# Three moves in a two-layer attention kernel: the last group of V's products in halves, half of the normalisation on ScalarE, output products from the last pair's third step

## The chip, the cores and the metric

The kernel runs on one core of a Trainium2 chip. The metric is the device time of one execution in microseconds (us), and lower is better. A core has TensorE (PE, matrix products into PSUM), VectorE (DVE), ScalarE (ACT), GpSimd (POOL) and SyncE (SP), which here only issues transfers. Each engine works off its own queue in order, and the engines meet at semaphores.

## The reference

Two layers run one after the other on x of 8 images, 512 channels and 32 x 32 places (T = 1024 tokens). Each is a group norm, a product for queries, keys and values, attention with 8 heads of 64, an output product, a bias and the residual. Cut to what matters:

```python
xn = group_norm(x, norm_w, norm_b)                 # 32 groups of 16 channels
q, k, v = split(qkv_w @ xn + qkv_b)                # per head: 64 channels each
weight = softmax(scale * q^T k)                    # 1024 x 1024 per image and head
a = weight @ v
out = x + proj_w @ a + proj_b
```

## The kernel before

**Passes.** One pass is one image in one layer, so the loop `Fori(0, PASSES)` runs 16 times on every engine. Within a pass the 8 heads go in 4 pairs. A head has 8 tiles of 128 queries, so a pair has 16 steps m = 0 to 15, one for each tile. Every fp32 product is made of three products of rounded parts (high by high, low by high, high by low), so operands are split into a high and a low part by ACT, POOL and DVE.

**One tile.** PE makes its scores (`scores`, L803 on, six matmuls, lines 812 and 814), DVE takes the row's smallest value (`smallest`, L600), ACT the exponential (`exponential`, L487), DVE the reciprocal of the row sum (L604), POOL multiplies by it (`normalise`, L373), PE transposes the tile (`transpose`, L823, eight matmuls into two halves of `ps_t`), ACT copies the high parts (`high_part`, L492), DVE subtracts for the low parts (`low_part`, L609), and PE weighs V with them (`weigh`, L835 and L836). PE's step with an even m first makes the scores of tiles m+2 and m+3. The scores of tile m+3 write the half of `ps_s` that the exponential of tile m+1 has read, so they wait for it.

**Start of a pass.** PE makes Q and K of head 0 (`qk_part`, 24 matmuls, channel block by channel block: block k waits for `xn_ready`), groups 0 to 3 of V (`values`, 12 matmuls each, one group for each 128 tokens), Q and K of head 1, and then groups 4 to 7 of V between the first scores. Group 7 stands between the transposes of tile 0 and those of tile 1 and goes to the bank `ps_o`. DVE copies each group out (`evac_v`, L673). ACT and POOL then split V for head 0 (`v_high` L481, `v_low` L367), and the first `weigh` waits for that.

**Boundary between passes.** Behind the last pair PE makes what is left of the eight output products (`project`, L775, in `OUT_ORDER`). Meanwhile DVE works out the group norm's coefficients of the next image (`norm_coefs`, ending at L663, `norm_b`). POOL then normalises the four blocks of 128 channels in place (`x_normalise`, L379), ACT copies each block's high part (`x_high`, L503), DVE subtracts for the low part (`x_low`, L668), and PE's next Q and K wait for it. Behind the four blocks ACT and POOL split blocks 2 and 3 of V's weights (`wv_high` L507, `wv_low` L346). Ahead of the first pass the same is written out by hand, and there ACT normalises blocks 1 and 3 (`x_normalise_first`, L516).

**Last pair.** In pairs 0 to 2 every step also makes three matmuls of the Q and K of a later head. The last pair has none to make. Its steps take the first nine matmuls of output product 6 instead, by the table `FILL`: step m makes the matmuls from the first to the second number. Step 4 first waits for the weights, for the last copy of Q and K out of the bank `ps_g`, which product 6 then fills, and for the attention of pairs 0 and 1. The scores of the last head (from tile 8 on, issued in step 6) wait for four transfers of its Q and K from one half of the partitions to the other (`stack`, L251 and L252). The loads of the next image are issued shortly before.

## Time and profile before

| | us |
|---|---|
| median of 3 runs | 4344.32 |
| lowest, highest | 4338.59, 4344.67 |
| the profiled execution's own time | 4335.69 |
| its span, first to last instruction | 4333.9 |

| engine | busy us | share of the span |
|---|---|---|
| PE | 4245.1 | 98% |
| DVE | 3305.3 | 76% |
| ACT | 2872.4 | 66% |
| POOL | 2436.4 | 56% |

The granted clock of TensorE is 0.999 of its full 2.4 GHz over the span. In the timelines a row begins with its start in us from the span's start and its duration; xN says that N neighbouring instructions of one kind are put together; brackets at the end give the idle time of the engine just before and what ended it. PEld is the weight load that runs ahead of a matmul.

### The profile page before, as it was taken

To read this page: it belongs to the slowest core of one execution; us is meant where nothing else is said; L and a number is where in the kernel's file an instruction comes from. 1 tells how busy PE (TensorE), PEld (TensorE's weight loads), DVE (VectorE), ACT (ScalarE), POOL (GpSimd) and SP (SyncE) were. 2 spreads that over 40 slices of the span, in tenths; PEclk is the share of its full clock that TensorE was granted. 3 is DMA by queue.
4 is the path that set the end of the run, shared out by engine and by line. 5 is a ranking of instruction groups with operands and counts; after the bars stand their busy time and mean duration, and the time that the engine had idled before them with its cause. 6 is when DMAs were issued, how large, how long until landed. Compare 5 with 4: busy or idle time off the path is not lost.

```text
span 4333.9 us, 94006 instructions
## 1 busy us (share of the span) xinstructions
PE 4245.1 (98%) x28740; PEld 3570.5 (82%) x28740; DVE 3305.3 (76%) x5479; ACT 2872.4 (66%) x5375; POOL 2436.4 (56%) x2332
## 2 busy tenths in 40 slices
PE   8999999999999999999999999999999999999999
PEld 6888888888887888878888788887888878888787
DVE  5878868688686886868868688686886868868687
ACT  4757747577574775747657476574765847658476
POOL 5646546465564655646566465564655646556464
PEclk9999999999999999999999999999999999999999
DMA  2121221212112121121221212122121211212112
GB/s 75 39 91 37 64 64 39 91 37 73 55 39 91 38 73 57 43 85 39 76 62 50 81 37 75 55 56 76 39 74 55 63 64 39 74 55 65 62 39 83
DMA packets 99645, 261.01 MB, mean 60 GB/s; under 512 B 15232, under 2 KB 15360, under 8 KB 99328
## 3 DMA queue, kind: packets, MB, share of 16 engines
q1 hardware_dynamic: 99328, 257.12, 20.0%
q8 instruction: 158, 2.59, 0.3%
q14 instruction: 159, 1.30, 0.1%
HBM read 122.84 MB, written 33.55 MB: 36 GB/s over the span
## 4 chain that ended last, share of the span: by engine, by line
PE 85%; POOL 4%; DVE 4%; issue 3%; DMA 2%; ACT 1%; SPq 1%; DVEq 0%; POOLq 0%; ACTq 0%
PE ps_t L823 20%; PE ps_s L812 17%; PE ps_g L775 15%; PE ps_o L835 10%; PE ps_o L836 10%; PE ps_s L775 6%; PE ps_t L775 4%; PE ps_o L775 2%; POOL x_raw L379 2%; DMA lo_sw<-lo_st 2%; PE ps_s L814 1%; DVE pt_lo L609 1%; DVE xn_lo L668 1%; POOL probs L373 0%; POOL v_st L367 0%
## 5 line engine op out<-in xcount | busy, mean ns | idle before, releaser
L373 POOL TENSOR_SCALAR probs<-probs,row_stats 128x1024 f32<-128x1024 f32 x1024 | 1153.0, 1126 | 1452.2 <-DVE row_stats L604 1452.1
L492 ACT CAST pt_hi<-ps_t 128x512 fp32r<-128x512 f32 x2048 | 1105.5, 590 | 759.6 <-PE ps_t L823 752.4
L600 DVE TENSOR_REDUCE row_stats<-ps_s 128x1 f32<-128x1024 f32 x1024 | 1249.2, 1220 | 296.5 <-PE ps_s L814 291.2
L609 DVE TENSOR_TENSOR pt_lo<-ps_t,pt_hi 128x512 fp32r<-128x512 f32 x2048 | 1317.3, 685 | 184.6 <-ACT pt_hi L492 171.8
L487 ACT ACTIVATE probs<-ps_s,row_stats 128x1024 f32<-128x1024 f32 x1024 | 1157.3, 1130 | 111.8 <-DVE row_stats L600 111.8
L823 PE MATMUL ps_t<-const_sb,probs 128*128 128x128 f32 x8192 | 1098.1, 276 | 5.1 <-POOL probs L373 4.8
L823 PEld LDWEIGHTS ps_t<-const_sb,probs 128*128 128x128 f32 x8192 | 898.6, 141 | 204.7 <-issue 179.5
L835 PE MATMUL ps_o<-pt_hi,v_st 128*128 128x256 f32 x4096 | 1023.6, 283 | 1.4
L836 PE MATMUL ps_o<-pt_lo,v_st 128*128 128x256 f32 x4096 | 1011.3, 281 | 0.0
L835 PEld LDWEIGHTS ps_o<-pt_hi,v_st 128*128 128x128 f32 x4096 | 770.1, 188 | 46.6 <-POOL v_st L367 8.3
L836 PEld LDWEIGHTS ps_o<-pt_lo,v_st 128*128 128x128 f32 x4096 | 772.0, 188 | 39.3
L812 PE MATMUL ps_s<-hi_sw,hi_st 64*128 64x512 f32 x1024 | 467.1, 456 | 44.5 <-DMA lo_sw<-lo_st 22.2
L814 PE MATMUL ps_s<-hi_st,hi_sw 64*128 64x512 f32 x1024 | 468.3, 457 | 0.0
L814 PE MATMUL ps_s<-hi_st,lo_sw 64*128 64x512 f32 x1024 | 405.2, 396 | 0.0
L812 PE MATMUL ps_s<-lo_sw,hi_st 64*128 64x512 f32 x1024 | 401.8, 392 | 0.0
L812 PE MATMUL ps_s<-hi_sw,lo_st 64*128 64x512 f32 x1024 | 399.3, 390 | 0.0
L814 PE MATMUL ps_s<-lo_st,hi_sw 64*128 64x512 f32 x1024 | 399.0, 390 | 0.0
L775 PE MATMUL ps_g<-xn_hi,wqk_hi 128*128 128x512 f32 x768 | 367.8, 479 | 0.0
L362 POOL TENSOR_TENSOR lo_st<-qk,hi_st 128x512 fp32r<-128x512 f32 x256 | 331.3, 1294 | 21.3
L812 PEld LDWEIGHTS ps_s<-hi_sw,hi_st 64*128 64x128 f32 x1024 | 188.2, 184 | 178.4 <-ACT probs L487 72.8
L775 PE MATMUL ps_g<-xn_hi,wqk_lo 128*128 128x512 f32 x768 | 305.2, 397 | 0.0
L775 PE MATMUL ps_g<-xn_lo,wqk_hi 128*128 128x512 f32 x768 | 301.8, 393 | 0.0
(125 smaller groups left out, 6397.3 us busy)
## 6 DMA issues: line engine op xcount, KB each, us to landing
wqk_raw<-in_wqk SPq DMA_DIRECT2D x130, 256.0 KB, 2.6
hi_sw<-hi_st SPq DMA_DIRECT2D x128, 256.0 KB, 3.1
lo_sw<-lo_st SPq DMA_DIRECT2D x128, 256.0 KB, 3.5
x_raw<-layer_out SPq DMA_DIRECT2D x36, 512.0 KB, 5.3
wv_raw<-in_wv SPq DMA_DIRECT2D x66, 256.0 KB, 5.2
x_raw<-in_x SPq DMA_DIRECT2D x32, 512.0 KB, 5.2
hi_sw<-hi_st SPq DMA_DIRECT2D x128, 128.0 KB, 3.1
lo_sw<-lo_st SPq DMA_DIRECT2D x128, 128.0 KB, 3.3
```

What stands on the lines that cost most here:

```text
L362: nc.gpsimd.tensor_tensor(lo_st[s][:, cols], qk[:, cols], f32(hi_st[s][:, cols]), ALU.subtract).then_inc(qk_split, 1)
L373: nc.gpsimd.tensor_scalar(probs[m % 2][:, :], probs[m % 2][:, :], row_rcp[:, m % 4:m % 4 + 1], 1.0, ALU.mult, ALU.mult).then_inc(probs_rea ...
L487: nc.scalar.activation(probs[m % 2][:, :], ps_s[:, m % 2, :], ACT.Exp, bias=row_min[:, m % 4:m % 4 + 1], scale=-1.0, accum_out=row_sum[:, ...
L492: nc.scalar.copy(pt_hi[:, m // 2 % 2, 4 * half:4 * half + 4, (m % 2) * P:(m % 2 + 1) * P], ps_t[:, half, :].rearrange("p (b t) -> p b t", ...
L600: nc.vector.tensor_reduce(row_min[:, m % 4:m % 4 + 1], ps_s[:, m % 2, :], AX.X, ALU.min).then_inc(min_ready, 1)
L609: nc.vector.tensor_tensor(pt_lo[place], ps_t[:, half, :].rearrange("p (b t) -> p b t", b=4), f32(pt_hi[place]), ALU.subtract).then_inc(lo_ ...
L775: return nc.tensor.matmul(bank, stat[hi_lo[0]](n // 3), mov[hi_lo[1]](n // 3), start=first, stop=last)
L812: nc.tensor.matmul(ps_s[:, m % 2, first], (hi_st, lo_st)[q][s][top, tile], (hi_sw, lo_sw)[k][s][top, first], start=n == 0, stop=n == 2)
L814: mm = nc.tensor.matmul(ps_s[:, m % 2, second], (hi_sw, lo_sw)[q][s][low, tile], (hi_st, lo_st)[k][s][low, second], start=n == 0, stop=n == 2)
L823: mm = nc.tensor.transpose(ps_t[:, half, b * P:(b + 1) * P], probs[m % 2][:, (4 * half + b) * P:(4 * half + b + 1) * P], ident)
L835: nc.tensor.matmul(ps_o[:, 0:GROUP], v, pt_hi[:, k % 2, b, :], start=(b == 0), stop=False)
L836: mm = nc.tensor.matmul(ps_o[:, 0:GROUP], v, pt_lo[:, k % 2, b, :], start=False, stop=(b == BLK - 1))
```

## The change

There are three edits. First, group 7 of V is made in two halves of six matmuls: the first between the transposes of tiles 0 and 1 as before, the second behind the transposes of tile 1. On DVE the copy of group 7 moves from ahead of step 1 to between the two low parts of step 1. Second, at every boundary ACT normalises blocks 1 and 3 and POOL only blocks 0 and 2. ACT's order there is normalise 1, high 1, high 0, normalise 3, high 3, high 2; DVE's low parts and PE's Q and K take the blocks in the order 1, 0, 3, 2 (`XN_ORDER`). The written-out start of the first pass becomes a call of the same helper. Third, `FILL` starts at step 2: two matmuls in steps 2 and 4, one in 6, 8 and 10, two in 12, nine in all as before; the three waits ahead of product 6 move from step 4 to step 2.

```diff
+XN_ORDER = [1, 0, 3, 2]
-FILL = {4: (0, 2), 6: (2, 4), 8: (4, 6), 10: (6, 8), 12: (8, 9)}
+FILL = {2: (0, 2), 4: (2, 4), 6: (4, 5), 8: (5, 6), 10: (6, 7), 12: (7, 9)}
...
@@ POOL, between passes
-                    for c in range(KT):
+                    for c in (0, 2):
                         x_normalise(i + 1, c)
...
@@ ACT
             def x_high(seq, c):
-                act.wait_ge(xn_f32, KT * seq + c + 1)
+                if c % 2 == 0:
+                    act.wait_ge(xn_f32, KT * seq + c + 2)
+                else:
+                    act.wait_ge(xn_f32_act, 2 * seq + c // 2 + 1)
                 nc.scalar.copy(xn_hi[:, c, :], x_raw[:, c, :]).then_inc(xn_hi_done, 1)
...
+            def x_normalise_odd(c):
                 nc.scalar.activation(x_raw[:, c, :], x_raw[:, c, :], ACT.Identity, bias=norm_b[:, c:c + 1],
-                                     scale=norm_a[:, c:c + 1]).then_inc(xn_f32_first, 1)
+                                     scale=norm_a[:, c:c + 1]).then_inc(xn_f32_act, 1)
+            def prepare_x(seq):
+                wait_alone(act, chain, CHAIN * (seq + 1))
+                for pair_of in range(2):
+                    x_normalise_odd(2 * pair_of + 1)
+                    x_high(seq, 2 * pair_of + 1)
+                    x_high(seq, 2 * pair_of)
...
-                    for c in range(KT):
-                        x_high(i + 1, c)
+                    prepare_x(i + 1)
...
@@ DVE
-            def x_low(seq, c):
-                dve.wait_ge(xn_hi_done, KT * seq + c + 1)
+            def x_low(seq, n):
+                c = XN_ORDER[n]
+                dve.wait_ge(xn_hi_done, KT * seq + n + 1)
...
                 low_part(tile + m, m, 0)
+                if begin and m == 1:
+                    evac_v(i, 7)
                 low_part(tile + m, m, 1)
...
-                step(i, lay, 0, 0, False)
-                evac_v(i, 7)
-                step(i, lay, 0, 1, False)
+                for m in range(2):
+                    step(i, lay, 0, m, False, True)
...
@@ PE
-                    if m == 4:
+                    if m == 2:
                         pe.wait_ge(wp_ready, KT * (i // B + 1))
                         pe.wait_ge(qk_evac, 2 * H * (i + 1))
                         pe.wait_ge(a_ready, a_at(PAIRS * i + 1, 3))
...
                 step(i, 0, 0)
-                values(7)
+                values(7, 0, 6)
                 step(i, 0, 1)
+                values(7, 6, 12)
```

DVE at the start of a pass, from the second low part of tile 0 (the write to `pt_lo`) to those of tile 1, before:

```order
L609 TENSOR_TENSOR pt_lo<-ps_t,pt_hi 128x4x128
L672 REGISTER_ALU
L673 COPY v_raw<-ps_o 128x512
L599 REGISTER_ALU
L600 TENSOR_REDUCE row_stats<-ps_s 128x1
L604 RECIPROCAL row_stats<-row_stats 128x1
L607 ISA
L609 TENSOR_TENSOR pt_lo<-ps_t,pt_hi 128x4x128
```

The same place in the changed kernel:

```order
L608 TENSOR_TENSOR pt_lo<-ps_t,pt_hi 128x4x128
L598 REGISTER_ALU
L599 TENSOR_REDUCE row_stats<-ps_s 128x1
L603 RECIPROCAL row_stats<-row_stats 128x1
L606 ISA
L608 TENSOR_TENSOR pt_lo<-ps_t,pt_hi 128x4x128
L672 REGISTER_ALU
L673 COPY v_raw<-ps_o 128x512
L606 REGISTER_ALU
L608 TENSOR_TENSOR pt_lo<-ps_t,pt_hi 128x4x128
```

The copy of group 7 (out of `ps_o`) moved behind the smallest value of tile 3, the reciprocal of tile 2 and the first low part of tile 1; the second low part of tile 1 now stands behind it.

ACT at the boundary, between its two stretches of V's weights (`wv_raw`, whose high parts lie in `pt_hi`), before, where four equal copies stand in a row:

```order
L507 CAST pt_hi<-wv_raw_55 128x512
L502 ISA
L503 CAST xn_hi<-x_raw 128x1024
L502 REGISTER_ALU
...
L226 ISA
L507 CAST pt_hi<-wv_raw_54 128x512
```

In the changed kernel:

```order
L510 CAST pt_hi<-wv_raw_55 128x512
L229 ISA
L519 ACTIVATE x_raw<-x_raw,norm_b,norm_a 128x1024
L506 CAST xn_hi<-x_raw 128x1024
L503 ISA
L506 CAST xn_hi<-x_raw 128x1024
L519 ACTIVATE x_raw<-x_raw,norm_b,norm_a 128x1024
L505 REGISTER_ALU
L506 CAST xn_hi<-x_raw 128x1024
L503 REGISTER_ALU
L506 CAST xn_hi<-x_raw 128x1024
L229 REGISTER_ALU
```

Two normalisations came in, each ahead of a pair of copies; of V's weights, block 2 now stands behind six instructions on x and no longer behind four.

## Rows read from the trace of the kernel before

**Rows 1.** The page, its part 1: busy time and share of each engine.
```profile
PE 4245.1 (98%) x28740; PEld 3570.5 (82%) x28740; DVE 3305.3 (76%) x5479; ACT 2872.4 (66%) x5375; POOL 2436.4 (56%) x2332
```

**Rows 2.** The view of waits: who waited for whom; us in total, times, longest.
```profile
PEld ps_s L812 <- ACT probs L487: 72.8, 104, 2.0
PEld ps_s L775 <- DVE xn_lo L668: 39.1, 41, 7.2
PE ps_s L812 <- DMA lo_sw<-lo_st: 22.2, 14, 3.7
```

**Rows 3.** Timeline of one boundary between passes: DVE, POOL and PE.
```profile
1091.68 0.16 DVE L663 TENSOR_TENSOR norm_b<-nb_sb,work 128x4 f32<-128x4 f32 x1
1092.06 6.78 POOL L379 TENSOR_SCALAR x_raw<-x_raw,norm_a,norm_b 128x1024 f32<-128x1024 f32 x4 [3.05 <-DVE norm_b L663]
1098.17 0.49 PE L775 MATMUL ps_s<-xn_hi,wqk_hi 128*128 128x512 f32 x1 [0.35 <-DVE xn_lo L668]
1101.24 0.50 PE L775 MATMUL ps_s<-xn_hi,wqk_hi 128*128 128x512 f32 x1 [0.29 <-DVE xn_lo L668]
```

**Rows 4.** Views of single lines: duration in ns, least, median and greatest.
```profile
L516 ACT ACTIVATE x_raw<-x_raw,norm_b,norm_a x2: 1240/1240/1240, 16.2 to 19.5; 128x1024 f32<-128x1024 f32 x2
L503 ACT CAST xn_hi<-x_raw x60: 1045/1054/1069, 286.4 to 4060.0; 128x1024 fp32r<-128x1024 f32 x60
L668 DVE TENSOR_TENSOR xn_lo<-x_raw,xn_hi x64: 1224/1234/2201, 18.7 to 4061.0; 128x1024 fp32r<-128x1024 f32 x64
```

**Rows 5.** Timeline of PE at a pass's start: group 7, tile 1, first scores, weighing.
```profile
1134.02 0.48 PE L775 MATMUL ps_o<-pt_hi,xn_hi 128*128 128x512 f32 x1
...
1136.86 1.04 PE L823 MATMUL ps_t<-const_sb,probs 128*128 128x128 f32 x8
...
1137.83 0.18 PEld L812 LDWEIGHTS ps_s<-hi_sw,hi_st 64*128 64x128 f32 x1 [0.17 <-issue]
...
1140.17 0.49 PE L812 MATMUL ps_s<-hi_sw,hi_st 64*128 64x512 f32 x1 [1.38 <-ACT probs L487]
...
1142.95 0.19 PEld L835 LDWEIGHTS ps_o<-pt_hi,v_st 128*128 128x128 f32 x1 [0.53 <-POOL v_st L367]
```

**Rows 6.** The same stretch on DVE, ACT and POOL.
```profile
1132.66 1.12 POOL L373 TENSOR_SCALAR probs<-probs,row_stats 128x1024 f32<-128x1024 f32 x1 [5.43 <-DVE row_stats L604]
1134.48 1.29 DVE L609 TENSOR_TENSOR pt_lo<-ps_t,pt_hi 128x512 fp32r<-128x512 f32 x2 [0.67 <-ACT pt_hi L492]
1137.06 0.69 DVE L673 COPY v_raw<-ps_o 128x512 f32<-128x512 f32 x1 [1.29 <-PE ps_o L775]
1137.50 1.08 ACT L492 CAST pt_hi<-ps_t 128x512 fp32r<-128x512 f32 x2 [1.46 <-PE ps_t L823]
1137.67 1.21 DVE L600 TENSOR_REDUCE row_stats<-ps_s 128x1 f32<-128x1024 f32 x1
1138.91 1.11 ACT L487 ACTIVATE probs<-ps_s,row_stats 128x1024 f32<-128x1024 f32 x1 [0.34 <-DVE row_stats L600]
1140.15 0.16 DVE L604 RECIPROCAL row_stats<-row_stats 128x1 f32<-128x1 f32 x1
1140.52 1.12 POOL L373 TENSOR_SCALAR probs<-probs,row_stats 128x1024 f32<-128x1024 f32 x1 [0.24 <-DVE row_stats L604]
1141.60 1.29 POOL L367 TENSOR_TENSOR v_st<-v_raw,v_st 128x512 fp32r<-128x512 f32 x1
```

**Rows 7.** Timeline of the last pair: transposes of tiles 2, 4, 8, 10, 14; scores.
```profile
1036.26 1.09 PE L823 MATMUL ps_t<-const_sb,probs 128*128 128x128 f32 x8
1042.25 1.09 PE L823 MATMUL ps_t<-const_sb,probs 128*128 128x128 f32 x8
1047.05 0.49 PE L812 MATMUL ps_s<-hi_sw,hi_st 64*128 64x512 f32 x1 [0.46 <-DMA lo_sw<-lo_st]
1054.75 1.09 PE L823 MATMUL ps_t<-const_sb,probs 128*128 128x128 f32 x8
1060.87 1.09 PE L823 MATMUL ps_t<-const_sb,probs 128*128 128x128 f32 x8
1072.26 1.09 PE L823 MATMUL ps_t<-const_sb,probs 128*128 128x128 f32 x8 [0.31 <-POOL probs L373]
```

**Rows 8.** ACT just ahead of the last pair's step 2: the last copy out of ps_g.
```profile
1035.60 0.77 ACT L474 ACTIVATE qk<-ps_g,bqk_sc,row_stats 128x512 f32<-128x512 f32 x1
```

More of the change, by code:

```diff
@@ L161, in build @@
         xn_f32 = sem("xn_f32")
-        xn_f32_first = sem("xn_f32_first")
+        xn_f32_act = sem("xn_f32_act")
         xn_hi_done = sem("xn_hi_done")
@@ L379, in x_normalise @@
                 nc.gpsimd.tensor_scalar(x_raw[:, c, :], x_raw[:, c, :], norm_a[:, c:c + 1], norm_b[:, c:c + 1],
-                                        ALU.mult, ALU.add).then_inc(xn_f32, 1)
+                                        ALU.mult, ALU.add).then_inc(xn_f32, 2)
             nc.gpsimd.memset(scratch[:, 4:6], 0.0).then_inc(a_ready, SPLIT_CREDIT)
@@ L384, in _ @@
             split_wqk(0, 0, 0)
-            wait_alone(pool, chain, CHAIN)
             for c in (0, 2):
-                nc.gpsimd.tensor_scalar(x_raw[:, c, :], x_raw[:, c, :], norm_a[:, c:c + 1], norm_b[:, c:c + 1],
-                                        ALU.mult, ALU.add).then_inc(xn_f32, 2)
+                x_normalise(0, c)
             for k in range(KT):
@@ L513, in attn_high @@
                                attn[:, cols].rearrange("p (o t) -> p o t", o=1)).then_inc(a_hi_done, 1)
-            def x_normalise_first(c):
+            def x_normalise_odd(c):
                 nc.scalar.activation(x_raw[:, c, :], x_raw[:, c, :], ACT.Identity, bias=norm_b[:, c:c + 1],
-                                     scale=norm_a[:, c:c + 1]).then_inc(xn_f32_first, 1)
-            act.wait_ge(chain, CHAIN)
-            x_normalise_first(1)
-            act.wait_ge(xn_f32, 2)
-            nc.scalar.copy(xn_hi[:, 0, :], x_raw[:, 0, :]).then_inc(xn_hi_done, 1)
-            act.wait_ge(xn_f32_first, 1)
-            nc.scalar.copy(xn_hi[:, 1, :], x_raw[:, 1, :]).then_inc(xn_hi_done, 1)
-            x_normalise_first(3)
-            act.wait_ge(xn_f32, 4)
-            nc.scalar.copy(xn_hi[:, 2, :], x_raw[:, 2, :]).then_inc(xn_hi_done, 1)
-            act.wait_ge(xn_f32_first, 2)
-            nc.scalar.copy(xn_hi[:, 3, :], x_raw[:, 3, :]).then_inc(xn_hi_done, 1)
+                                     scale=norm_a[:, c:c + 1]).then_inc(xn_f32_act, 1)
[5 more added lines that the diff above has]
+                    x_high(seq, 2 * pair_of)
+            prepare_x(0)
             act.wait_ge(setup_done, 2)
@@ L703, in _, with step @@
             nc.vector.tensor_scalar(bqk_sc[:, :], bqk_sb[:, :], qk_scale[:, :], None, ALU.mult).then_inc(setup_done, 1)
-            def step(i, lay, p, m, last):
+            def step(i, lay, p, m, last, begin=False):
                 pair = PAIRS * i + p
@@ L777, in qk_part @@
             def qk_part(half, bank, s, lo, hi):
-                stat = (lambda k: wqk_hi[s][:, k, :], lambda k: wqk_lo[s][:, k, :])
-                mov = tuple((lambda k, xn=xn: xn[:, k, half * HALF:(half + 1) * HALF]) for xn in (xn_hi, xn_lo))
+                stat = (lambda n: wqk_hi[s][:, XN_ORDER[n], :], lambda n: wqk_lo[s][:, XN_ORDER[n], :])
+                mov = tuple((lambda n, xn=xn: xn[:, XN_ORDER[n], half * HALF:(half + 1) * HALF]) for xn in (xn_hi, xn_lo))
                 for n in range(lo, hi):
```

## The prediction

> **What bounds the kernel now.** I read the page's busy times first. PE is busy for 98% of the span and no other engine for more than 76% [rows 1], so PE's own queue is the path to the end. The change adds and removes no matmul, so it can win only what PE waits. The view of waits says where that is: scores wait for ACT's exponential, the first product of a pass waits for the low part of the normalised input, and scores of the last pair wait for a transfer [rows 2]. The timelines then show these three places in the pass, which repeats 16 times with 15 boundaries between: four blocks at each make the 60 copies of line 503 [rows 4]. At a boundary POOL normalises four blocks in a row, and PE starts the fourth block only at 1101.24 [rows 3]. At the start of a pass PE waits 1.38 for the exponential of tile 3 and 0.53 ahead of the first weighing [rows 5]. In the last pair two steps take 5.99 or 6.12, with or without matmuls to fill them, and a transfer comes late [rows 7].
>
> **Normalising on two engines.** The coefficients are ready at 1091.68 + 0.16 = 1091.84. PE begins the fourth block 1101.24 - 1091.84 = 9.40 later [rows 3]. In the changed order ACT does two normalisations of 1.24 (the first pass has just this instruction) and four copies of 1.05. The third copy, of block 3, ends 2 x 1.24 + 3 x 1.05 = 5.63 after the coefficients, the two low parts that are then left take 1.23 each on DVE [rows 4], which makes 8.09, and with 0.06 for the hand-overs PE begins its fourth block after 8.15. The gain is 9.40 - 8.15 = 1.25. DVE's low parts of blocks 1 and 0 are done by about 2.29 + 2 x 1.23 = 4.75, before PE comes, and POOL's two blocks need about half of its 6.78, so block 0 is there when ACT asks for it. ACT idles there until POOL's first block is done, so the added 2.48 lie where it waits now. Of what is queued behind, V's weights of blocks 2 and 3 are needed only after 24 matmuls of Q and K. PE could not gain much more: the first block began at 1098.17 with 0.35 idle, and nine matmuls at 2.84 / 12 = 0.237 [rows 5] end 2.13 later, so without any wait the fourth block would start at 1097.82 + 2.13 = 1099.95, a gain of 1.29. I take 1.25 x 15 = 18.8 us. The lower end is 0.27 a boundary (the port rival below). The start of the first pass has the same six instructions in another order and I cost it at nothing, within 0.5 us either way.
>
> **V's last group in halves.** Group 7 takes 1136.86 - 1134.02 = 2.84, a half 1.42. Tile 1's transposes can then begin at 1135.44. What they need is there: tile 1 is normalised by 1132.66 + 1.12 = 1133.78, and tile 0's low parts end at 1134.48 + 1.29 = 1135.77, the first half of them some 0.64 sooner, and only the second half of the transposes waits for the later one [rows 5, 6]. So everything that hangs on tile 1's transposes comes 1.42 sooner. On DVE the smallest value of tile 3 no longer stands behind the copy of group 7: it ends at about 1135.77 + 1.21 = 1136.98 instead of 1138.88. ACT's two copies of tile 1 end at 1137.50 + 1.08 - 1.42 = 1137.16, the exponential takes 1.11 and a readout, so it ends near 1138.5, and the scores of tile 5, which follow those of tile 4 (still at 1137.83, since the same matmuls stand ahead) by 0.9, no longer wait for it. That frees 1.38. What is late next is the first weighing. It waits for V's low part on POOL (1141.60 + 1.29), which stands behind POOL's work on tile 3 (1140.52), and that waits for DVE's reciprocal (1140.15) [rows 6]. In the changed order this reciprocal follows the copy of group 7 and one low part. The second half of the group ends where the loop's branch begins, at 1137.83 - 0.17 = 1137.66; the copy came 0.20 behind its matmuls (1137.06 against 1136.86), so it runs from 1137.86 to 1138.55, the low part (1.29 / 2) ends at 1139.20, and the reciprocal comes 0.95 sooner. DVE's wait for the second half of the group holds up this low part and the reciprocal alone. POOL and the weighing move by the same 0.95; I take 0.9, since a wait for V's low part now stands alone in front of PE: 0.9 x 16 = 14.4 us. The ends are 0, if the copy out of `ps_o` is held up as long as the reciprocal gains, and 1.38 + 0.53 = 1.91 a pass, if neither wait remains.
>
> **Output products from step 2.** Two steps with two matmuls to fill take 1060.87 - 1054.75 = 6.12, with none 1042.25 - 1036.26 = 5.99 [rows 7]. So another engine sets most of the time, and a step with one matmul lies between; I take the middle, 6.05. Steps 6, 8 and 10 lose one matmul each, 3 x 0.07 = 0.21 a pass. Step 12 gets one more, 0.237, and tile 14's transposes wait 0.31 for POOL just behind [rows 7], so it costs nothing; without that cover it would cost 0.24. Step 2 gets two: 5.99 becomes 6.12. In the 14 passes where the last head's scores wait for their transfer [rows 2], this 0.13 is waited away; in the other two it counts. The wait moved to step 2 is covered: the last copy out of `ps_g` ends at 1035.60 + 0.77 = 1036.37 [rows 8], the products come behind the transposes, 0.85 after 1036.26. If it were late, the weighing of tile 2 and the scores of tile 6 on PE would be held up. Sum: -0.21 x 16 + 0.13 x 2 = -3.1 us, between -0.13 x 3 x 16 = -6.2 and, with both added matmuls of step 2 uncovered, +0.47 x 16 = +7.6.
>
> **The sum.** -18.8 - 14.4 - 3.1 = -36.3 us. The profiled execution took 4335.69 with a span of 4333.9, so 1.8 lie outside it and stay. It would take 4335.7 - 36.3 = 4299.4. The median of the runs before, 4344.32, is 8.6 above the profiled execution, so I forecast 4299.4 + 8.6 = 4308.
>
> **Rivals.** *POOL takes the port.* A low part of x takes 1.23 at its least and 2.20 at its greatest [rows 4], and in between POOL is at work on the same rows. If POOL's subtraction for V's weights (block 2) came ahead of the last low part, that low part would be 0.98 later, 14.7 us over 15 boundaries: 4323. For it: POOL has only two blocks now and is ready sooner. Against it: that subtraction waits for ACT's copy behind the last copy of x, while the last low part waits only for the latter. I give it 6 in 100. The Trainium skill, "SBUF — State Buffer", section "Who interferes with whom", says that a DVE instruction with two SBUF inputs and a GpSimd instruction that reads SBUF exclude each other for a whole instruction, and that whichever starts first holds the port. By that rule the 0.98 is the price, and the order of the two starts decides; the spread from 1.23 to 2.20 agrees with it.
>
> *The halves gain nothing.* The wait of 1.38 goes, but the weighing comes where it came before, since POOL's part of V is late by other work: 4308 + 14.4 = 4322. For it: V's low part is the last in a chain of DVE, POOL and PE whose slack is not seen. Against it: each link moves with the one ahead [rows 6]. 7 in 100.
>
> *Slower: the transfers of the last head come later still.* PE waits for them 22.2 us in 14 passes, 1.4 a pass over 16, at most 3.7 [rows 2]. They share the queues with the next image. Nothing in the change issues a transfer earlier relative to the last pair's start, but if shorter passes moved them under more traffic, it would undo the gain: from a mean of 1.4 + 36.3 / 16 = 3.7 on there is none, and from 4.2 a pass on the kernel is slower by over 0.2%; a mean of 4.5 would make 4308 + 3.1 x 16 = 4358. That is beyond the longest wait seen. 3 in 100.
>
> *No change:* the first two rivals together, 4308 + 14.7 + 14.4 = 4337, with no further loss, 4 in 100. That the edits do not do what they say is excluded by the built order.
>
> **How the numbers follow.** The forecast has 80 in 100. The range goes from 4295 (all three gains at 1.2 times and the runs as near to their fastest as before) to 4323, which takes in the first two rivals. Faster or slower by 0.2%, about 8.7 us, is what a measurement of this kernel can tell from no change. Forecast and the first two rivals are faster (93 in 100), the double rival the same (4), the transfers slower (3).
>
> **What would show it.** Right: PE's fourth block of Q and K about 8.15 after `norm_b` instead of 9.40; POOL's L379 group with two instructions a boundary and the wait of ACT's copies for it nearly gone; no wait of the scores of tile 5 for the exponential, and a longer one of the first weighing for V's low part, near 0.5 + 1.38 - 0.9 = 1.0; two steps of the last pair near 6.05; the wait for the transfer shorter by about 0.1 a pass. Wrong: a low part of 2.2 in the last place at a boundary, the reciprocal of tile 3 at its old distance from the copy of group 7, a wait of PE ahead of product 6 in step 2, or a sum of transfer waits far from 22 us.

## The result, and the profile of the changed kernel

The changed kernel takes 4304.47 us (median of 4 runs, 4302.03 to 4306.98), the kernel before 4343.36 in the same comparison (4338.59 to 4344.67). The ratio is 0.9912, with a 95% interval from 0.9895 to 0.9930: faster by 0.9%, as forecast (4308, range 4295 to 4323). The profiled execution of the changed kernel took 4303.43 with a span of 4301.6, that is 32.3 less than the one before.

The page's busy line of the changed kernel answers to [rows 1]: ACT has gained 35 us of work, POOL has lost 63, and PE keeps its 28740 matmuls.

```profile
PE 4231.6 (98%) x28740; PEld 3571.8 (83%) x28740; DVE 3284.8 (76%) x5479; ACT 2907.0 (68%) x5405; POOL 2373.7 (55%) x2302
```

Its view of waits (us in total, times, longest) answers to [rows 2]. The wait for the exponential has halved, the one for the low parts of x has gone but for the first pass (9.0 of its 12.7), the one for the transfer is as it was. Two have grown: the weighing's wait for V's low part (8.3 before) and, ahead of Q and K, "issue" (1.9 before), time in which PE waited for nothing that the profile shows.

```profile
PEld ps_s L813 <- ACT probs L487: 36.5, 85, 1.7
PE ps_s L813 <- DMA lo_sw<-lo_st: 24.1, 16, 4.1
PEld ps_o L836 <- POOL v_st L370: 18.3, 16, 1.2
PEld ps_s L776 <- DVE xn_lo L668: 12.7, 7, 9.0
PEld ps_s L776 <- issue: 9.7, 14, 0.9
```

The boundary of [rows 3] now reads, on DVE, ACT, POOL, DVE, PE. POOL's group has two instructions, ACT works without a gap, DVE's last low part ends at 1089.34 + 2.36 = 1091.70, which is 8.05 behind the coefficients (1083.49 + 0.16). PE begins its first block at 1090.10 with 0.47 idle and no releaser, its fourth (the tenth matmul) at 1092.28, 8.63 behind the coefficients.

```profile
1083.49 0.16 DVE L662 TENSOR_TENSOR norm_b<-nb_sb,work 128x4 f32<-128x4 f32 x1
1083.78 1.26 ACT L519 ACTIVATE x_raw<-x_raw,norm_b,norm_a 128x1024 f32<-128x1024 f32 x1 [5.21 <-DVE norm_b L662]
1088.25 2.00 ACT L506 CAST xn_hi<-x_raw 128x1024 fp32r<-128x1024 f32 x2
1083.87 2.41 POOL L382 TENSOR_SCALAR x_raw<-x_raw,norm_a,norm_b 128x1024 f32<-128x1024 f32 x2 [3.04 <-DVE norm_b L662]
1089.34 2.36 DVE L668 TENSOR_TENSOR xn_lo<-x_raw,xn_hi 128x1024 fp32r<-128x1024 f32 x2 [0.82 <-ACT xn_hi L506]
1090.10 0.49 PE L776 MATMUL ps_s<-xn_hi,wqk_hi 128*128 128x512 f32 x1 [0.47 <-issue]
1092.28 0.39 PE L776 MATMUL ps_s<-xn_hi,wqk_hi 128*128 128x512 f32 x1
```

The start of the same pass answers to [rows 5, 6]: PE's two halves of group 7 around tile 1's transposes, the scores of tile 5 (1129.56) straight behind those of tile 4, the weighing with its wait; then DVE's copy of group 7 and the reciprocal of tile 3, and POOL's work on tile 3 and on V.

```profile
1124.92 0.48 PE L776 MATMUL ps_o<-pt_hi,xn_hi 128*128 128x512 f32 x1
1126.40 1.03 PE L824 MATMUL ps_t<-const_sb,probs 128*128 128x128 f32 x8
1127.19 0.47 PE L776 MATMUL ps_o<-pt_hi,xn_hi 128*128 128x512 f32 x1
1128.76 0.50 PE L813 MATMUL ps_s<-hi_sw,hi_st 64*128 64x512 f32 x1
1129.56 0.39 PE L813 MATMUL ps_s<-hi_sw,hi_st 64*128 64x512 f32 x1
1132.84 0.19 PEld L836 LDWEIGHTS ps_o<-pt_hi,v_st 128*128 128x128 f32 x1 [1.15 <-POOL v_st L370]
...
1128.87 0.69 DVE L673 COPY v_raw<-ps_o 128x512 f32<-128x512 f32 x1 [0.40 <-PE ps_o L776]
1130.07 0.15 DVE L603 RECIPROCAL row_stats<-row_stats 128x1 f32<-128x1 f32 x1
...
1130.43 1.12 POOL L376 TENSOR_SCALAR probs<-probs,row_stats 128x1024 f32<-128x1024 f32 x1 [1.22 <-DVE row_stats L603]
1131.51 1.28 POOL L370 TENSOR_TENSOR v_st<-v_raw,v_st 128x512 fp32r<-128x512 f32 x1
```

PE is the path to the end, so its queue can be cut into stretches, each from the start of its first matmul to that of the next stretch, and summed over the 16 passes. The sums in us, up to PE's last matmul, worked out from PE's records in each profile (the experiments are told below; the 4.2 from that matmul to the end of the span are left out):

| stretch of PE | before | after | e1 halves | e2 boundary | e3 fill | e5 v_low | e10 loads | e12 before, loads | e11 all |
|---|---|---|---|---|---|---|---|---|---|
| start, first 24 matmuls | 30.3 | 31.9 | 33.1 | 33.7 | 31.0 | 31.8 | 31.8 | 32.7 | 30.6 |
| product 5 to the next 24 matmuls | 151.2 | 134.0 | 150.6 | 135.9 | 151.4 | 133.8 | 133.3 | 152.1 | 133.2 |
| group 7 to the end of the first pair's round | 960.8 | 944.8 | 944.8 | 960.8 | 960.9 | 928.9 | 944.8 | 960.9 | 928.6 |
| last pair, steps 2 to 14 | 654.6 | 653.9 | 664.0 | 673.4 | 657.4 | 661.4 | 628.7 | 630.5 | 628.6 |
| everything else | 2532.8 | 2532.9 | 2532.9 | 2532.8 | 2532.9 | 2532.8 | 2532.9 | 2532.9 | 2532.2 |

So the 32.3 consist of 17.2 at the boundaries, 16.0 at the passes' starts and 0.6 in the last pair, less 1.6 lost at the start of the first pass. The last row says that nothing else moved. The first row also differs among kernels that begin alike (30.3 to 33.1 in the kernel before, e1, e3 and e12), and the fourth differs by up to 19.5 us among kernels that issue the same transfers; the experiments say why.

### The profile page after: what moved, and what is told of

It is laid out like the page before. It is cut to its first block, busy times and chain, and to the rows that moved or that the text cites. A ratio compares the mean times of both kernels' runs of the same rounds, so it can differ in the third digit from the quotient of the medians.

```text
span 4301.6 us, 94022 instructions
## 1 busy us (share of the span) xinstructions
PE 4231.6 (98%) x28740; PEld 3571.8 (83%) x28740; DVE 3284.8 (76%) x5479; ACT 2907.0 (68%) x5405; POOL 2373.7 (55%) x2302
## 4 chain that ended last, share of the span: by engine, by line
PE 90%; issue 2%; DMA 2%; POOL 2%; ACT 2%; DVE 1%; SPq 1%; POOLq 0%; ACTq 0%; DVEq 0%
PE ps_t L824 20%; PE ps_s L813 17%; PE ps_g L776 15%; PE ps_o L836 10%; PE ps_o L837 10%; PE ps_s L776 8%; PE ps_t L776 6%; PE ps_o L776 3%; DMA lo_sw<-lo_st 2%; PE ps_s L815 1%; ACT probs L487 1%; POOL a_lo L400 1%; POOL lo_st L365 0%; POOL v_st L370 0%; SPq L254 0%
## 5 line engine op out<-in xcount | busy, mean ns | idle before, releaser
L836 PEld LDWEIGHTS ps_o<-pt_hi,v_st 128*128 128x128 f32 x4096 | 770.6, 188 | 59.0 <-POOL v_st L370 18.3
L813 PE MATMUL ps_s<-hi_sw,hi_st 64*128 64x512 f32 x1024 | 465.1, 454 | 24.1 <-DMA lo_sw<-lo_st 24.1
```

The lines of the kernel that those rows point to most:

```text
L813: nc.tensor.matmul(ps_s[:, m % 2, first], (hi_st, lo_st)[q][s][top, tile], (hi_sw, lo_sw)[k][s][top, first], start=n == 0, stop=n == 2)
L836: nc.tensor.matmul(ps_o[:, 0:GROUP], v, pt_hi[:, k % 2, b, :], start=(b == 0), stop=False)
```

## Each edit alone

**e1: the halves alone,** on the kernel before, with DVE's copy of group 7 between the low parts of step 1 as in the change.

```diff
...
-                values(7)
+                values(7, 0, 6)
                 step(i, 0, 1)
+                values(7, 6, 12)
```

> The kernel before with V's last group in halves alone. Theory (the three edits win at three separate places and add up): PE's stretch from tile 0's transposes to the end of pair 0 is 1.0 us shorter in each of 16 passes, a span near 4333.9 - 16 = 4318, and the boundary stays as it was. Rival (the halves pay only because the pass begins sooner after the boundary): no change, 4334.

Measured: 4336.51 against 4349.68, ratio 0.9969 (0.9957 to 0.9982). The stretch from group 7 on is 16.0 shorter, to the tenth of a us what it is in the whole change; the boundaries stay. The weighing waits 18.3 us for V's low part, 1.14 a pass. The halves' gain is their own.

**e2: the boundary alone,** with group 7 and `FILL` as before.

```diff
+XN_ORDER = [1, 0, 3, 2]
...
-                    for c in range(KT):
+                    for c in (0, 2):
                         x_normalise(i + 1, c)
...
```

> The kernel before with the normalisation on two engines alone, the start of the first pass included. Theory: PE's fourth block of Q and K begins 8.1 to 8.7 after the coefficients instead of 9.4 to 9.6, about 1.15 us at each of 15 boundaries, and the first pass begins 2.0 later, so 4333.9 - 17.2 + 1.6 = 4318. Rival (ACT's new work at the boundary delays what follows on ACT, its copies of V's weights and of Q): less than half of it, 4326 or more.

Measured: 4336.48 against 4349.68, ratio 0.9963 (0.9946 to 0.9980). The boundaries take 15.3 less, 1.02 each; DVE's last low part ends 8.03 to 8.05 behind the coefficients at every one of the 15, but PE's fourth block begins only 8.57 behind them in the mean. The start of the first pass has lost, as in the changed kernel. The profile's span (4340.8) hides the gain, since steps 4 and 6 of the last pair took 18.8 more than in the profile of the kernel before: PE waits 31.2 us for the transfers instead of 22.2, and behind these waits its granted clock fell in eight passes instead of three (shown at e10).

**e3: the table alone.**

```diff
-FILL = {4: (0, 2), 6: (2, 4), 8: (4, 6), 10: (6, 8), 12: (8, 9)}
+FILL = {2: (0, 2), 4: (2, 4), 6: (4, 5), 8: (5, 6), 10: (6, 7), 12: (7, 9)}
...
-                    if m == 4:
+                    if m == 2:
```

> The kernel before with the new table of output products alone. Theory (another engine sets the step time, one matmul less gives 0.13 a step in steps 8 and 10, and step 2, 12 and 14 give it back): between -4 and +2 us, 4330 to 4336, apart from the transfers' own scatter. Rival (the early matmuls hide the last head's transfer): the sum of PE's waits for that transfer falls by 5 us or more, 4328.

Measured: ratio 0.9995 (0.9978 to 1.0012), no difference that can be told. By steps (medians over 16 passes): step 2 from 5.80 to 5.87, steps 8 and 10 from 6.12 to 5.99, step 12 from 5.95 to 5.97, step 14 from 3.25 to 3.31. The three ratios together leave 0.9927, inside the interval of the whole change, so the edits add up.

## Where the boundary stopped short

DVE's part came out as worked out (8.05 against 8.09), yet PE was late by up to 0.7. In the changed kernel the time from the first matmul of product 5 to the first of the next pass is 2.72 at its least and 2.78 to 3.40 at 14 of the 15 boundaries. The records show an instruction load of 16 KB (queue q8) that begins some 0.2 before product 5; at the one boundary with 2.72 it took 1.22, at most others 1.5 to 1.8. What goes with the delay is when the load ends: 1.0 behind product 5's first matmul at the boundary with 2.72, 1.1 to 1.2 at those with 2.78 and 2.84, 1.2 to 1.6 where it is 3.05 to 3.40 (one of these loads took only 0.92, but began 0.6 behind that matmul). The same happened at 10 boundaries of the kernel before, where the wait for the low parts hid it. Two experiments test that.

**e8: the stores held back.** The stores of the output run at the same time as that load. Here all four wait for the last output product.

```diff
-                    wait_alone(sp, out_ready, out_at(i, 2 * o + 1))
+                    wait_alone(sp, out_ready, out_at(i, OUT_ORDER[-1]))
```

> The changed kernel, where SP stores the output blocks only when all eight output products are done. Theory (PE begins a pass 0.4 late because the instructions at the head of its loop are loaded through the same transfer engines as the stores and the loads of V's weights): the loads of instructions near the boundary take 1.2 instead of 1.5 to 1.8, product 5 is followed by the next pass after 2.72 at nearly all boundaries instead of one of 15, and PE's fourth block is bound by DVE at 8.1 instead of 8.4: about 3 us, 4299. Rival (PE's wait at the loop's head has another cause): 2.8 to 3.4 as in the changed kernel, 4302.

Measured: the load takes 0.88 to 0.98 at 11 boundaries, where product 5 takes 2.72, and 1.18 to 1.39 at the other four, where it takes 2.74 to 2.92. The fourth block begins 8.08 to 8.10 behind the coefficients at 14 of the 15, so the boundary gains 1.35 and not 1.15. The whole is no faster (4310.83, ratio 0.9909, 0.9892 to 0.9925): in the last pass the stores now stand at the end, and the span ends 8.1 instead of 4.2 behind PE's last matmul, and the transfers of the last pair took 27.2 us of waiting.

**e9: TensorE's loop over two passes,** the same instructions in the same order. At seven of the 15 boundaries PE then takes the loop's back edge, the branch from its end to its head; at the other eight it goes straight on.

```diff
-            with pe.Fori(0, PASSES) as i:
-                hd0 = H * i
+            with pe.Fori(0, PASSES // 2) as twice:
+                for odd in range(2):
+                    i = 2 * twice + odd
+                    hd0 = H * i
...
```

> The changed kernel with TensorE's loop written out over two passes: eight rounds of two passes, the same instructions in the same order, so that at eight of the 15 boundaries PE goes straight on and at seven it goes back to the loop's head. In the changed kernel the time from the first matmul of product 5 to the first of the next pass is 2.72 at its least and 2.78 to 3.40 at 14 of 15 boundaries. Theory (the instruction load at the loop's back edge makes PE late): at the eight straight boundaries 2.72 to 2.76, at the seven back edges 2.8 to 3.4, alternating; the fourth block of Q and K about 8.1 after norm_b at the straight ones and 8.1 to 8.7 at the others. Rival (PE is late there because of its own waits, for the low parts, for the copies out of the banks, or the shared transfers whatever the loop): no alternation, 2.8 to 3.4 nearly everywhere.

Measured: 2.72 at all eight boundaries without a branch, and 3.40, 3.32, 3.49, 3.39, 3.38, 3.02, 3.00 at the seven back edges between them. At the eight there is no instruction load near product 5, at the seven there is one of 1.5 to 1.8 (once 0.88, begun 0.7 behind product 5). PE at a back edge (the last matmul of a pass, the first of the next) and, below the dots, at the straight boundary behind it:

```profile
557.98 0.39 PE L776 MATMUL ps_t<-a_hi,wp_lo 128*128 128x512 f32 x1
558.88 0.49 PE L776 MATMUL ps_s<-xn_hi,wqk_hi 128*128 128x512 f32 x1 [0.52 <-issue]
...
829.10 0.39 PE L776 MATMUL ps_t<-a_hi,wp_lo 128*128 128x512 f32 x1
829.33 0.39 PE L776 MATMUL ps_s<-xn_hi,wqk_hi 128*128 128x512 f32 x1
```

The page's row on the instruction queue (packets, MB, share) has 158 loads in the changed kernel and, last, 150 here, eight fewer for eight back edges fewer:

```profile
q8 instruction: 158, 2.59, 0.3%
```
```profile
q8 instruction: 150, 2.46, 0.3%
```

At the straight boundaries the fourth block begins 8.08 to 8.10 behind the coefficients. The theory of the back edge stands, and its price is 0.3 on a mean boundary. One run of 4308.51 says nothing of the time, since the transfers scatter by more.

**e6: the port.** ACT's copy for V's weights of block 2 comes ahead of its last copy of x, so that POOL's subtraction meets DVE's last low part. That is the first rival made true.

```diff
                     x_high(seq, 2 * pair_of + 1)
+                    if pair_of == 1 and between is not None:
+                        between()
                     x_high(seq, 2 * pair_of)
...
-                    prepare_x(i + 1)
-                    for k in range(2, KT):
-                        wv_high(i + 1, k)
+                    prepare_x(i + 1, lambda: wv_high(i + 1, 2))
+                    wv_high(i + 1, 3)
```

> The changed kernel, where ACT copies the high part of V's weights, block 2, ahead of the last copy of x, so that POOL's subtraction is ready before DVE's last low part. Theory (DVE's and POOL's instructions on SBUF operands exclude each other, whichever starts first runs to its end): POOL's subtraction starts first and takes 1.3, DVE's last low part takes about 2.2 instead of 1.22, PE's fourth block begins near 9.4 to 9.7 after the coefficients instead of 8.4, some 15 us more in all, 4316. Rival (they share, or DVE goes first): the last low part ends only 0.6 later, with the delayed copy, and the span is at most 5 us longer.

Measured, one run: 4322.44. DVE's last two low parts, then POOL's two subtractions, at one boundary:

```profile
1092.49 1.23 DVE L669 TENSOR_TENSOR xn_lo<-x_raw,xn_hi 128x1024 fp32r<-128x1024 f32 x1 [0.80 <-ACT xn_hi L506]
1093.96 2.00 DVE L669 TENSOR_TENSOR xn_lo<-x_raw,xn_hi 128x1024 fp32r<-128x1024 f32 x1 [0.24 <-ACT xn_hi L506]
...
1093.06 4.04 POOL L349 TENSOR_TENSOR pt_lo<-wv_raw,pt_hi 128x512 fp32r<-128x512 f32 x2 [3.61 <-ACT pt_hi L510]
```

POOL has started first, and the low part takes 2.00 instead of 1.23. It ends 1.09 later than in the changed kernel at all 15 boundaries, and PE's stretch is 13.5 us longer. Of the 1.09, 0.31 is the edit's own, since ACT's extra copy makes the low part start later, and 0.78 is the meeting with POOL. So the rival's price was somewhat high (0.98 each, 14.7 in all; 0.78 gives 11.7). In the changed kernel the two instructions meet as well, the other way round:

```profile
1090.86 3.25 POOL L349 TENSOR_TENSOR pt_lo<-wv_raw,pt_hi 128x512 fp32r<-128x512 f32 x2 [4.58 <-ACT pt_hi L510]
```

POOL's first subtraction starts here 0.38 behind DVE's last low part (1090.48, the second of the two at 1089.34) and itself takes 1.99, where the second takes 1.29; at all 15 boundaries it is 0.37 or 0.38, and 1.99 or 2.00. The rival did not come because the order of the two starts is as argued, by that margin. This is what the Trainium skill, "SBUF — State Buffer", section "Who interferes with whom", states of a DVE instruction with two inputs in SBUF and one of GpSimd that reads there: one waits for the other. The trace agrees, with 2.00 against 1.23 for DVE and 1.99 against 1.29 for POOL.

## The first pass and the weighing

**e4: the first wait attached to its instruction.** The changed kernel's helper puts a wait of its own ahead of ACT's normalisation; the kernel before had the wait on the instruction. Here the first pass has it so again.

```diff
-            def prepare_x(seq):
-                wait_alone(act, chain, CHAIN * (seq + 1))
+            def prepare_x(seq, apart=True):
+                if apart:
+                    wait_alone(act, chain, CHAIN * (seq + 1))
+                else:
+                    act.wait_ge(chain, CHAIN * (seq + 1))
...
-            prepare_x(0)
+            prepare_x(0, False)
```

> The changed kernel, where ACT's first instruction of the first pass waits for the coefficients itself instead of through a separate wait ahead of it. Theory (the load of ACT's table, 1.28 us, stands behind the separate wait and so behind the coefficients; before, it ran at 0.7 us): the table loads near 0.7 again, PE's first block starts near 20.0 to 20.4 instead of 21.9, the span is 1.5 us shorter than the changed kernel's, 4300. Rival (the new order of the six instructions costs the time): no change, 21.9.

Measured, ACT and PE at the start, first of the changed kernel, then of e4:

```profile
16.37 1.28 ACT L519 ACT_TABLE_LOAD   x1 [16.37 <-DVE norm_b L662]
17.66 1.24 ACT L519 ACTIVATE x_raw<-x_raw,norm_b,norm_a 128x1024 f32<-128x1024 f32 x1
21.94 0.80 PE L776 MATMUL ps_s<-xn_hi,wqk_hi 128*128 128x512 f32 x1 [8.96 <-DVE xn_lo L668]
```
```profile
0.74 1.28 ACT L519 ACT_TABLE_LOAD   x1 [0.74 <-PEq L1008]
17.41 1.24 ACT L519 ACTIVATE x_raw<-x_raw,norm_b,norm_a 128x1024 f32<-128x1024 f32 x1 [15.38 <-DVE norm_b L665]
21.08 0.79 PE L779 MATMUL ps_s<-xn_hi,wqk_hi 128*128 128x512 f32 x1 [6.99 <-DVE xn_lo L671]
```

The first ACT instruction with a function brings a load of its table. In the changed kernel it stands behind the separate wait, when the coefficients are already there; in e4 it is done at 2 us. The coefficients end at 16.26 and 17.37 (the first loads landed at different times), so PE begins 5.68 and 3.71 behind them, and its fourth block 10.99 and 9.02. The seven other profiles with the separate wait show 10.97 or 10.98. The loss is 1.96 us, once. ACT's normalisation begins 1.40 instead of 0.04 behind the coefficients, which makes 1.36 of it; the rest comes where DVE's low parts stand beside POOL's instructions on V's weights (the first takes 1.87 instead of 1.27, the third 2.30 instead of 1.87).

Measured from the kernel before, the loss is not one number. There the fourth block begins 9.12 behind the coefficients in the kernel's own profile, but 10.28 or 10.29 in e1, e3 and e12, whose first pass is the same. DVE's first low part starts 2.52 behind the coefficients and POOL's copy of V's weights 0.03 or 0.04 later; in the kernel's own profile the low part takes 1.23 and the copy 1.66, in e1 the low part 1.72 and the copy 0.62. So the changed kernel's 10.97 to 10.99 is 1.9 or 0.7 later, which goes with how the two met.

The time of e4 (4318.5, ratio 0.9945, 0.9927 to 0.9964) does not show the gain; steps 4 and 6 took 11.9 more in this profile than in that of the changed kernel.

**e5: V's low part first.** On POOL the low part of V for head 0 moves ahead of the normalisation of tile 3.

```diff
-                for m in range(2):
-                    step(i, 0, m, False)
+                step(i, 0, 0, False)
                 v_low(hd0, 0, 0)
+                step(i, 0, 1, False)
```

> The changed kernel, where POOL makes the low part of V for head 0 ahead of tile 3's normalisation instead of behind it. Theory (in the changed kernel the first weighing waits only for POOL's queue: reciprocal of tile 3, its normalisation 1.12, then V's low part): the wait of PE for V's low part, some 1.0 a pass, goes, and pair 0 takes 0.7 to 1.0 less, a span of 4301.6 - 11 to -16 = 4286 to 4290. Rival (DVE's copy of group 7 and ACT's copy of V are what the weighing waits for): less than 0.3 a pass, 4297 or more.

Measured: 4295.37 against 4353.27, ratio 0.9876 (0.9859 to 0.9892). POOL at a pass's start:

```profile
1130.86 1.27 POOL L370 TENSOR_TENSOR v_st<-v_raw,v_st 128x512 fp32r<-128x512 f32 x1 [1.09 <-ACT v_st L481]
1132.12 1.13 POOL L376 TENSOR_SCALAR probs<-probs,row_stats 128x1024 f32<-128x1024 f32 x1
```

No wait of PE for V's low part is left, the stretch is 15.9 us shorter, and the first pair's round now takes what the second does (867.6 and 867.8 over 16 passes). Tile 3's transposes do not miss their operand. The wait into which the halves turned a part of their gain was an order on POOL, worth 1.0 a pass.

## The last pair

**e7: all nine matmuls in steps 2 and 4.**

```diff
-FILL = {2: (0, 2), 4: (2, 4), 6: (4, 5), 8: (5, 6), 10: (6, 7), 12: (7, 9)}
+FILL = {2: (0, 6), 4: (6, 9)}
...
-                    if m == 10:
+                    if m == 4:
                         pe.wait_ge(a_ready, a_at(PAIRS * i + 2, 3))
```

> The changed kernel with six of the nine early output products in step 2 and three in step 4, none in steps 6 to 12. Theory (other engines set the step time at 5.8 to 6.0 whatever fills it, and the wait for the last head's transfer, 24 us in all, is hidden under the matmuls ahead of it): step 2 grows by up to 0.8, the wait for the transfer falls by about 0.8 a pass or 10 us in all, and steps 6 to 12 gain 0.1 each: a span of 4290 to 4298. Rival (matmuls in step 2 delay the chain of tile 3 to 5, and PE gets no slack in front of the transfer): 4302 to 4308.

Measured: ratio 0.9910 (0.9894 to 0.9927), as the changed kernel. Step 2 takes 6.80, so four more matmuls cost 0.93, 0.23 each. Steps 8 and 10 without a matmul take 5.99 and 6.00: as with one (5.99), where two take 6.12. A step carries one for nothing. PE waits 10.2 us for the transfer, in 7 passes, and the steps 2 to 14 take 657.5 against 653.9: what the wait loses, the matmuls have taken.

**e10: the next image's loads behind the last head's transfers.** In every kernel so far SP issues the image's four loads ahead of the four transfers for which the last head's scores wait. Here they wait for these to land.

```diff
+                load_wqk(next_layer * H + 1, 1)
+                stack(hd0 + H - 1, 1)
+                wait_alone(sp, stacked[1], 64 * (PAIRS * i + PAIRS))
                 with sp.If(nxt < B):
                     load_x(x, within(nxt, 0, B - 1))
...
-                load_wqk(next_layer * H + 1, 1)
-                stack(hd0 + H - 1, 1)
```

> The changed kernel with one move on SP: the four loads of the next image stand behind the last head's four transfers and wait until these have landed; the residual and V's weights, which follow in SP's order, come later with them. The image is read by the statistics some 30 us later. Theory A (the last head's transfers come late because the next image's 2 MB and the loads behind share the queues with them): the wait of the scores for the transfer falls from 24.1 us in the profile of the changed kernel to under 5, step 4 with what hangs on it from a mean of 7.70 to 6.1, step 6 stays at 5.78 in all passes, and the time falls by 20 to 30 us against the changed kernel, to a ratio of 0.984 to 0.987 against the kernel before. Theory B (the transfer's own latency from its issue, 3.0 us at the least, and its late issue make PE wait): the wait stays at 20 us or more and the ratio at 0.991.

Measured: 4278.77 against 4352.08, ratio 0.9831 (0.9803 to 0.9859). SP's issues (the image, the last transfer) and PE's transposes of tiles 2, 4 and 6 in one last pair, first of the changed kernel, then of e10:

```profile
1025.31 1.92 SPq L239 DMA_DIRECT2D x_raw<-in_x  x4
1033.58 0.60 SPq L255 DMA_DIRECT2D lo_sw<-lo_st  x1
...
1033.35 1.09 PE L824 MATMUL ps_t<-const_sb,probs 128*128 128x128 f32 x8
1039.13 0.49 PE L813 MATMUL ps_s<-hi_sw,hi_st 64*128 64x512 f32 x1 [1.44 <-DMA lo_sw<-lo_st]
1040.73 1.09 PE L824 MATMUL ps_t<-const_sb,probs 128*128 128x128 f32 x8
1046.72 1.09 PE L824 MATMUL ps_t<-const_sb,probs 128*128 128x128 f32 x8
```
```profile
1032.59 0.60 SPq L255 DMA_DIRECT2D lo_sw<-lo_st  x1
1036.19 2.04 SPq L239 DMA_DIRECT2D x_raw<-in_x  x4
...
1032.44 1.09 PE L825 MATMUL ps_t<-const_sb,probs 128*128 128x128 f32 x8
1038.56 1.09 PE L825 MATMUL ps_t<-const_sb,probs 128*128 128x128 f32 x8
1044.54 1.09 PE L825 MATMUL ps_t<-const_sb,probs 128*128 128x128 f32 x8
```

No wait for a transfer is left. Step 4 takes 6.12 in all 16 passes (6.35 to 10.32 in the changed kernel), step 6 takes 6.04. Step 6 is not the 5.78 that was expected: that value was itself what followed a delayed step 4. The last transfer is issued 0.15 behind tile 2's transposes, and 0.23 in the changed kernel, so its issue has hardly moved: the image's traffic, not the transfer's own latency, made PE wait.

A late transfer costs more than its wait. In the 12th and 13th pass of the changed kernel PE waits 4.13 and 3.65 for it, and then its granted clock is at the lower of its two levels, 1.2 GHz. One of the two waits, with a matmul of 0.79 behind it where others take 0.39 to 0.50, and a stretch shortly after (its length, the busy time of PE, PEld, DVE, ACT and POOL, then the granted clock, 0.50):

```profile
3443.66 0.79 PE L813 MATMUL ps_s<-hi_sw,hi_st 64*128 64x512 f32 x1 [3.65 <-DMA lo_sw<-lo_st]
3444.00:3449.00 5.00, 5.00 (x23) 3.88 (x22) 2.30 (x3) 1.07 (x3) 0.00 (x0) 0.50 0.05 18
```

In these two passes the last pair takes 5.35 and 6.10 longer than in e10, 3.7 more than the waits; in the other 14 it loses no more than the wait. In e10, e11 and e12 the clock is full in the last pair of every pass.

**e12: the same move alone on the kernel before.**

> The kernel before with one edit: the next image's loads behind the last head's four transfers, waiting until these have landed. None of the change's three edits is in. Theory (the waits for these transfers are the same burden in both kernels, and the change's own gains lie elsewhere): steps 4 and 6 of the last pair are alike in all 16 passes, no wait for a transfer is left, the time is 4310 to 4316, ratio 0.990 to 0.993, and against the changed kernel with the same move (4278.8) the change's three edits are worth 32 to 36 us, as in the profiles. Rival (part of the measured gain came from the transfers, which a shorter pass happened to move): the two differ by under 28 or by over 40.

Measured: 4313.93 against 4348.22, ratio 0.9917 (0.9898 to 0.9936). Its four runs lie between 4313.02 and 4315.05, where the nine of the kernel before beside them lie between 4342.76 and 4362.66: the waits and the clock behind them are also most of what makes the runs differ (the granted clock over the run is 1.000 in e12's four, 0.997 to 0.999 in the nine). Against e10 the change is worth 35.2 us, and the two ratios, 0.9831 / 0.9917 = 0.9913, give what the change gave without the move (0.9912). With the transfers out of the way, the last pair shows the table alone: 630.5 against 628.7, a gain of 1.9.

**e11: e4, e5 and e10 together.**

> The changed kernel with three edits at once: the next image's loads behind the last head's transfers, POOL's low part of V for head 0 ahead of its work on tile 3, and the first normalisation's wait fused, so that the table of functions is loaded early. Theory (the three gains lie at different places of PE's queue and add up): the stretch of PE from step 2 of the first pair on takes 54.2 a pass instead of 55.2, the steps 4 and 6 of the last pair 6.12 and 6.04 in all 16 passes, the fourth block of the first pass 9.0 instead of 11.0 behind the coefficients; against the changed kernel with the loads moved alone, which took 4278.8, the time falls by 16 + 2 to 4261, a ratio of 0.979 against the kernel before. Rival (a shorter pass brings the last head's transfers or the stores under more traffic and gives part of it back): 4268 or more, with waits of PE for a transfer over 5 us in sum.

Measured: 4260.23 against 4348.22, ratio 0.9795 (0.9779 to 0.9811), faster than either kernel. Each stretch has the value that its own experiment gave it (the table above), so nothing is given back.

## Why the prediction was right, and where it was not

The forecast's own sum was 36.3; the two profiles differ by 32.3, the medians by 38.9, and with the transfers out of the way in both (e12 against e10) by 35.2. The mechanisms were right at the boundary and in the halves, less so in the table; that the sum came so close is partly luck, since the halves gained 1.6 more, which makes up for the 1.6 by which the boundaries fell short. Step by step:

- **Boundary, 18.8 forecast, 17.2 measured.** The chain of ACT and DVE is right to 0.05, and with no instruction load in the way the fourth block begins 8.08 to 8.10 behind the coefficients, as the 8.15 of the prediction said. The step that failed is the sentence that PE could come without idle time: the 0.35 idle ahead of the first block [rows 3] was taken for the wait that it names. In PE's and DVE's records that low part ends 3.78 behind the coefficients and PE begins 6.33 behind them, so PE waited for something else; its loop head is late at most boundaries anyway.
- **Start of the first pass, nothing within 0.5 forecast, 1.6 lost** in the two profiles, where the first loads differ; behind the coefficients it is 1.9 (0.7 against e1, e3 and e12), and e4 gives back 1.96. "The same six instructions in another order" overlooked that the helper's wait is an instruction of its own and that the table's load stands behind it; the low parts' meetings with POOL were left out as well.
- **Halves, 14.4 forecast, 16.0 measured.** Every link moved as worked out: the reciprocal by 0.98 (0.95 forecast; 5.15 instead of 6.13 behind group 7's first matmul), the weighing by 1.01. I had taken 0.9 for fear of the separate wait; the weighing moved by the full 1.0. The wait that is left is 1.15, near the 1.0 named.
- **Table, 3.1 forecast, 0.6 in the two profiles, 1.9 with the transfers away.** Steps 8 and 10 gained more than the middle I chose (0.13, not 0.07), since the first matmul in such a step is free (e7). Step 2's added 0.07 counts in all 16 passes and not in two, and steps 4, 12 and 14, for which the prediction had set down nothing, lose 0.13 together (e10 against e12); in the two profiles the transfers' scatter covers the rest.
- **The median above the profiled execution, 8.6 forecast, 1.0 measured.** The profiled execution of the kernel before was its shortest (4335.69, the others from 4338.59 on); how long the others waited for transfers no profile shows. Taking its distance to the median over to the changed kernel was no step that a row supported. By it alone the forecast would have been 7.6 too high; the sum, which promised 4.0 too much, took half of that back, and the median came out 3.5 below the forecast. That these two errors worked against each other is luck.

Of the rivals, the port was real, at 0.78 a boundary instead of 0.98 (e6), and its condition did not occur. The halves gained. The transfers of the last head, the slower rival, made PE wait 24.1 us against 22.2, where about 0.1 a pass less was forecast; this moved little, but what they cost in either kernel is more than any of the three edits gained: 24.1 us of the last pair before (654.6 against 630.5 in e12) and 25.2 after (653.9 against 628.7 in e10), the fallen clock included.

## What to carry to other kernels

When a wait on the path is taken away, look for what stood behind it unseen: here a loop's back edge and a subtraction on another engine had been hidden by it, and each took back a part of the gain. Cut the queue of the engine that bounds the kernel into stretches and compare their sums; a change of 0.4% shows there to a tenth of a us while transfers make whole runs differ by 20. A transfer that an engine needs in a few us goes ahead of bulk loads that nobody reads for 30, and these wait until it has landed (in the changed kernel the image's loads are issued from 1025.31 on, and DVE reads the image first at 1066.49).

## What the runs showed of the hardware

A branch back to the head of TensorE's loop brings an instruction load of 16 KB. It takes 0.9 with the stores held back (e8) and costs nothing then; at 1.5 to 1.8, beside the stores, PE comes 0.3 to 0.7 late. It also came late at the one back edge of e9 where the load took 0.88 but began 0.7 behind product 5. Without the branch there is no such load (e9). ACT's load of its table, 1.28, goes ahead of the first instruction that needs it but behind a wait that stands as an instruction of its own (e4). The Trainium skill, "ScalarE: Activation LUTs", section "What ACT_TABLE_LOAD costs", has about 1283 ns for such a load, and the rows here show the same. A subtraction on DVE and one on POOL, both on two inputs in SBUF, do not run at once: whichever starts second takes about 2.0 instead of 1.2 or 1.3 (e6 and the changed kernel). PE's granted clock fell to 1.2 GHz in some of the last pairs in which it had waited for a late transfer, and in none without such a wait (e10). Not tried was a boundary without any back edge, with the loop written out in full, nor a table that gives every step just one matmul.
